# One stationary matrix for the last gate and up columns of a feed-forward layer

## What is computed

```
gate = x @ Wg + bg                     # Wg, Wu: 256 x 682
up   = x @ Wu + bu
ffn  = (silu(gate) * up) @ Wd + bd     # Wd: 682 x 256
return layer_norm(x + ffn, g2, b2)
```

## Time and profile before

| | |
|---|---|
| profiled execution | 1076.54 us |
| its span, first to last instruction | 1074.8 us |
| median of three timed runs | 1077.23 us |
| TensorE busy | 900.4 us, 84% of the span |
| VectorE busy | 768.5 us, 72% |
| GpSimd busy | 414.9 us, 39% |
| the feed-forward stage | from 428.7 to 575 us |

### The profile page before, as it was taken

The page is one execution under the profiler, slowest core; times in us unless marked ns, Lnnn a source line. Parts: engine busy times, 40 slices in busy tenths (PEclk is TensorE's granted clock), DMA queues, the critical chain, the costliest instruction groups (busy, mean ns, idle before and its releaser), DMA issues. The chain is left out here.

```text
span 1074.8 us, 17848 instructions
## 1 busy us (share of the span) xinstructions
PE 900.4 (84%) x5607; PEld 766.1 (71%) x5616; DVE 768.5 (72%) x1474; ACT 378.0 (35%) x712; POOL 414.9 (39%) x480
## 2 busy tenths in 40 slices
PE   3399999999847764889876789877499999999998
PEld 1399999999836663778764655436288888888887
DVE  5788888888639799676667666446647777777776
ACT  4366655666223311222124255556411111111110
POOL 3177787778500242543243732300022232332332
PEclk9699999999969886899888899988799999999999
DMA  7346123242160000600003920000011001010102
GB/s 262 105 135 197 44 61 105 87 145 97 40 219 1 0 1 0 189 1 1 1 1 60 181 64 1 2 1 1 0 30 30 16 28 29 15 29 15 29 0 78
DMA packets 50300, 61.81 MB, mean 58 GB/s; under 512 B 8014, under 2 KB 37768, under 8 KB 50248
## 3 DMA queue, kind: packets, MB, share of 16 engines
q1 hardware_dynamic: 43464, 43.85, 13.2%
q0 software_dynamic: 6336, 17.31, 6.7%
q10 hardware_dynamic: 448, 0.01, 0.0%
HBM read 47.26 MB, written 7.60 MB: 51 GB/s over the span
## 5 line engine op out<-in xcount | busy, mean ns | idle before, releaser
L2273 POOL TENSOR_TENSOR e_hl<-e_h32sb,e_hh 128x512 fp32r<-128x512 f32 x68 | 88.1, 1295 | 283.5 <-DVE e_hh L2297 283.5
L2264 ACT ACTIVATE e_silusb<-psum 128x512 f32<-128x512 f32 x68 | 40.7, 598 | 242.7 <-PE psum L2217 242.7
L2305 DVE SCALAR_TENSOR_TENSOR y<-psum,comb,y 128x256 f32<-128x256 f32 x272 | 112.2, 475 | 0.0
L2294 DVE TENSOR_TENSOR e_h32sb<-psum,e_silusb 128x512 f32<-128x512 f32 x68 | 47.0, 692 | 85.1 <-PE psum L2217 71.7
L443 ACT ACTIVATE e_u<-psum,e_bias 128x256 f32<-128x256 f32 x152 | 63.8, 471 | 95.8 <-PE psum L342 94.7
L2217 PE MATMUL psum<-act_hi,e_w0h 128*128 128x512 f32 x144 | 58.1, 404 | 9.8 <-ACTq L2257 9.8
L1274 POOL TENSOR_TENSOR ff_hl<-ff_h32sb,ff_hh 128x512 fp32r<-128x512 f32 x24 | 34.5, 1440 | 71.1 <-DVE ff_hh L1309 71.1
L1863 DVE TENSOR_REDUCE at_mn<-psum 128x4 f32<-128x512 f32 x64 | 42.9, 688 | 26.5 <-PE psum L1535 26.2
L2217 PE MATMUL psum<-act_hi,e_w0l 128*128 128x512 f32 x144 | 57.4, 399 | 0.0
L2217 PE MATMUL psum<-act_lo,e_w0h 128*128 128x512 f32 x144 | 57.2, 397 | 0.0
L352 PE MATMUL psum<-e_w3h,e_h2h 128*128 (+1 forms) x160 | 47.8, 299 | 8.2 <-issue 7.8
(11 more groups left out here) (504 smaller groups left out, 3211.5 us busy)
## 6 DMA issues: line engine op xcount, KB each, us to landing
e_raw<-in_W SPq DMA_DIRECT2D x16, 512.0 KB, 6.8
e_raw<-in_W SPq DMA_DIRECT2D x8, 1024.0 KB, 5.8
y<-in_x SPq DMA_DIRECT2D x4, 512.0 KB, 9.6
v_tok<-in_xT SPq DMA_DIRECT2D x4, 512.0 KB, 8.1
y<-y_rows SPq DMA_DIRECT2D x4, 512.0 KB, 6.9
v_tok<-y_rows SPq DMA_DIRECT2D x4, 512.0 KB, 7.8
v_tok<-in_x SPq DMA_DIRECT2D x4, 512.0 KB, 9.1
e_raw<-in_w_gate SPq DMA_DIRECT2D x16, 128.0 KB, 2.2
```

The lines of the kernel that those rows point to most:

```text
L2264: act.activation(sl_sb[:, s % 2, :], ps[s % 2][:, :], ACT.Silu).then_inc(sil, 1)
L2273: pool.tensor_tensor(hh[1][:, s % HS, :], h32[:, s % 2, :], hh[0][:, s % HS, :], ALU.subtract).then_inc(hsp, 1)
L2294: dve.tensor_tensor(h32[:, s % 2, :], ps[2 + s % 2][:, :], sl_sb[:, s % 2, :], ALU.mult).then_inc(h32d, 1)
L2305: dve.scalar_tensor_tensor(out=y[:, i, :], in0=ps[4 + j][:, 0:D], scalar=comb[:, i, bass.ds(2 * t + out_s // G, 1)], in1=y[:, i, :], op0=A ...
```

## The change

Steps of the last piece get a stationary matrix of their own, `wr` (high and low): columns 0 to 41 are the gate's last 42 columns, columns 64 to 105 the up part's, the rest zeros. `up(s)` of such a step runs one set of six products into the gate bank, where the gate's values then lie on rows 0 to 41 and the up part's on rows 64 to 105. ScalarE, VectorE and GpSimd work on 42 rows in these steps, VectorE's product reading its first factor from PSUM row 64 on. In `down`, the three products of the last piece contract over 42 rows in place of 128. The weights' preparation is cut accordingly: two blanks over the whole of `wr` in place of four over the spare columns, and for each of gate and up a rounding and a subtraction of the first 640 columns and another pair for the 42.

```diff
+                wg = [sbl(f"ff_wg{h}", [P, KC, FULL], F32R) for h in "hl"]
+                wu = [sbl(f"ff_wu{h}", [P, KC, FULL], F32R) for h in "hl"]
+                wr = [sbl(f"ff_wr{h}", [P, KC, P], F32R) for h in "hl"]
+                rows_of = lambda m: P if m < FC - 1 else FR
...
                     def up(s):
                         g, m = s // FC, s % FC
+                        if m == FC - 1:
+                            pe.wait_ge(sil, s - 1)
+                            for n, (k, (a, b)) in enumerate((k, p) for k in range(KC) for p in PASSES):
+                                last = pe.matmul(ps[s % 2], wr[a][:, k, :], actT[b][:, k, g * GT:(g + 1) * GT],
+                                                 start=n == 0, stop=n == 3 * KC - 1)
+                            last.then_inc(hps, 2)
+                            return
...
-                                pe.wait_ge((sil, h32d)[v], s - 1)
+                                pe.wait_ge(sil if v == 0 and (s - 2) % FC < FC - 1 else h32d, s - 1)
...
-                                last = pe.matmul(ps[4 + i % 2][:, 0:D], hh[a][:, m, j * P:(j + 1) * P],
-                                                 wd[b][:, m, :], start=n == 0, stop=n == 3 * FC - 1)
+                                last = pe.matmul(ps[4 + i % 2][:, 0:D], hh[a][0:rows_of(m), m, j * P:(j + 1) * P],
+                                                 wd[b][0:rows_of(m), m, :], start=n == 0, stop=n == 3 * FC - 1)
...
-                        pool.tensor_tensor(hh[1][:, m, :], h32[:, s % 2, :], hh[0][:, m, :],
+                        nr = rows_of(m)
+                        pool.tensor_tensor(hh[1][0:nr, m, :], h32[0:nr, s % 2, :], hh[0][0:nr, m, :],
...
-                        for wt in (wg, wu):
-                            last = dve.memset(wt[part][:, :, F:FC * P].bitcast(F32), 0.0)
+                        last = dve.memset(wr[part][:, :, :].bitcast(F32), 0.0)
...
-                        weights_split(dve, ch, [(raw[n][:, :, :], wt[0][:, :, 0:F], wt[1][:, :, 0:F])], wsp)
+                        rest = [v[:, :, n * UP_AT:n * UP_AT + FR] for v in wr]
+                        dve.tensor_copy(wt[0][:, :, :], raw[n][:, :, 0:FULL])
+                        ch.link(dve.tensor_copy(rest[0], raw[n][:, :, FULL:F]))
+                        dve.tensor_tensor(rest[1], raw[n][:, :, FULL:F], rest[0], ALU.subtract)
+                        dve.tensor_tensor(wt[1][:, :, :], raw[n][:, :, 0:FULL], wt[0][:, :, :], ALU.subtract).then_inc(wsp, 1)
...
-                        dve.scalar_tensor_tensor(out=h32[:, s % 2, :], in0=ps[2 + s % 2],
-                                                 scalar=bu[:, m:m + 1], in1=sl_sb[:, s % 2, :],
+                        product = ps[2 + s % 2] if m < FC - 1 else ps[s % 2][UP_AT:UP_AT + nr, :]
+                        dve.scalar_tensor_tensor(out=h32[0:nr, s % 2, :], in0=product,
+                                                 scalar=bu[0:nr, m:m + 1], in1=sl_sb[0:nr, s % 2, :],
```

More of the change, by code:

```diff
@@ L1146, in stage_feed_forward @@
                 rawd = sbl("ff_rawd", [P, FC, D])
-                wg = [sbl(f"ff_wg{h}", [P, KC, FC * P], F32R) for h in "hl"]
-                wu = [sbl(f"ff_wu{h}", [P, KC, FC * P], F32R) for h in "hl"]
+                FULL = (FC - 1) * P
+                UP_AT = P // 2
+                assert FR <= UP_AT
+                wg = [sbl(f"ff_wg{h}", [P, KC, FULL], F32R) for h in "hl"]
+                wu = [sbl(f"ff_wu{h}", [P, KC, FULL], F32R) for h in "hl"]
+                wr = [sbl(f"ff_wr{h}", [P, KC, P], F32R) for h in "hl"]
                 wd = [sbl(f"ff_wd{h}", [P, FC, D], F32R) for h in "hl"]
@@ L1255, in _ @@
                             act.wait_ge(h32d, s - 1)
-                        act.activation(sl_sb[:, s % 2, :], ps[s % 2], ACT.Silu,
-                                       bias=bg[:, m:m + 1]).then_inc(sil, 1)
+                        act.activation(sl_sb[0:rows_of(m), s % 2, :], ps[s % 2][0:rows_of(m), :], ACT.Silu,
+                                       bias=bg[0:rows_of(m), m:m + 1]).then_inc(sil, 1)
                         if g and m == 2:
@@ L1308, in hidden @@
                             dve.wait_ge(ops, (s // FC) * TG)
-                        dve.tensor_copy(hh[0][:, m, :], h32[:, s % 2, :]).then_inc(hhi, 1)
+                        dve.tensor_copy(hh[0][0:nr, m, :], h32[0:nr, s % 2, :]).then_inc(hhi, 1)
                     def lo(g):
```

## The result

The changed kernel takes 1089.62 us (median of 4 runs, 1089.46 to 1091.97) against 1077.03 for the kernel before (1075.09 to 1077.29): a ratio of 1.0126, 95% interval 1.0108 to 1.0144. It is slower by some 12.6 us. The forecast was 1081.0 and its range ended at 1084.5: right in sign, far too small.

The account below looks back on a forecast made before the run. It took VectorE's chain, then GpSimd, then `down` as the bound. Removed products 0, changes of rows +2.8, clock +1.0 and other edits 0 gave +3.8 on 1077.23: 1081.0 us, range 1076.8 to 1084.5.

Parts of the forecast that it names:

- The 24 products are worth nothing: Gate and up sets: 5.4 us of TensorE's time go, hidden by VectorE's chain in all four groups; counted 0.
- The other edits (GpSimd and VectorE on 42 rows, the preparation): Product, silu, rounding and subtraction on 42 rows, and the weights' preparation: no change in time, counted 0.
- A change of rows costs 0.09 us at the full clock: In `down`, each change between 128 and 42 rows; 0.14 us at the low clock, 28 changes, together +2.8 us.
- Rival B: In `down`, changes of rows cost 0.19 us or more throughout: 6.3 us in all, 1083.5 us; chance 0.13.
- In each other group the first 3 to 5 us of `down` ran at the low clock: `down` after group 0: two changes of rows at 0.14 us, five at 0.09; 0.73 us, three times 2.2.
- the clock's term of +1.0: Longer idle stretches of TensorE bring the low clock earlier in `down(0)` and group 1: 0.75 and 0.27 us, between 0 and 2.
- groups 2 and 3 start `down` at the low clock already: `down` of groups 2 and 3: already at the low clock at its start, so no added clock loss counted.
- The chance of the low clock in `down(0)`: `down(0)` may begin at the low clock after 3.0 us idle: even odds of 1.5 us, counted 0.75.
- The sign: Whole kernel: slower by more than 0.2% (2.15 us), chance 0.65; the same 0.29, faster 0.06.

## Why the prediction was wrong

- *The 24 products are worth nothing:* right. TensorE's idle time took them, and with `down` at 128 rows the stage did not get shorter.
- *The other edits (GpSimd and VectorE on 42 rows, the preparation):* right, within 0.3 us. The subtraction takes 1.26 us as before, and from the stage's first blank to its first product it is 3.26 us against 3.34.
- *A change of rows costs 0.09 us at the full clock:* too low. I read only the step into the new product. The product behind it is late as well, so a change costs 0.19 at the full clock and about 0.3 at the low one, where I had 0.14. With the clock held high all changes cost 5.8 us, where I had 2.8. Rival B, decided "from 0.15 us a change on", had this term nearly right, 5.3, with the same +1.0 for the clock. Its reason, a full weight load behind each change, fits the trace: at a change the load starts together with its product and not 0.12 us ahead, and the next product is 0.11 late. No run varied the load, so it stays an argument.
- *"In each other group the first 3 to 5 us of `down` ran at the low clock", taken over unchanged; and the clock's term of +1.0, of which "groups 2 and 3 start `down` at the low clock already" made nothing:* this failed, and it is the larger part. I asked when the clock falls and took for granted when it rises. Before, TensorE in `down` works without a break and the low clock lasts 3.4 to 5.1 us; with a block of 42-row products every 15 full ones it lasted 8 to 12.7. That cost 7.1 us where I had 1.0. That the 42-row blocks do it is shown, by taking them out and by putting them in alone; by what means is not. The chance of the low clock in `down(0)` did not come true in the profiled execution of the changed kernel, and did in all five kernels that clear two tiles and use 128, 96 or 72 rows.
- *The range:* each bound was set for a term by itself. But both terms hang on the same 42-row products, so they came out high together, and the low clock makes each change dearer. The sign was right for part of the reason only: 5.8 of the 12.9 us are the mechanism that I named.

## What to carry to other kernels

Contract over all 128 rows of a zero-padded last piece, or over 72 or 96 of them, rather than over 42 between full ones: the short products save no time (0.28 us, as the full ones), and every change of rows makes two products late. Where TensorE begins a burst at the low clock, ask what lets the clock rise again: in an unbroken run of products it did so within 3 to 5 us here, in a run with three 42-row products behind every 15 full ones it took up to 12.7. If short products can't be avoided, put them next to each other (11 us of the loss went by reversing every second tile's order). And if TensorE waits ahead of a burst on the path, products that nobody reads can hold the clock: 1077 to 1069.5 us here, a ratio of 0.9945 (0.9928 to 0.9962).

## What was not expected of the hardware

- A change between 128 and 42 rows costs 0.08 us on the first product and 0.11 on the second at 2.4 GHz; between 128 and 72 or 96 rows nothing.
- With three 42-row products behind every 15 full ones, the clock stayed at 1.2 GHz for up to 52 products in a row, 12.7 us of `down(1)`, with TensorE never idle by the profile. At the full clock the same pattern did not make it fall.
- In the filled kernel before, `down(1)` and `down(2)`, behind filling products, took 8.27 us, `down(0)`, behind an idle stretch, 8.56, all at the full clock: 0.115 us from start to start against 0.119.
- GpSimd's subtraction takes 1.26 us on 42 rows as on 128, VectorE's product 0.75, ScalarE's silu 0.68 against 0.69.
- The kernel before varies more than its first three runs showed: 1071.9 to 1078.6 over all runs.
